# A recommendation model's pair products: eight bursts of 32 small matmuls a part become four of 64

## The reference

```python
fm = emb_table[jnp.arange(N_CAT)[None, :], cat_idx]
h = jax.nn.relu(dense_x @ Wd1 + bd1)
h = jax.nn.relu(h @ Wd2 + bd2)
dense = jax.nn.relu(h @ Wdf + bdf)
Z = jnp.concatenate([fm, dense[:, None, :]], axis=1)
S = jnp.einsum('bie,bje->bij', Z, Z)
iu, ju = np.triu_indices(N_CAT + 1, k=1)
x = jnp.concatenate([S[:, iu, ju], dense], axis=-1)
x = jax.nn.relu(x @ Wt1 + bt1)
x = jax.nn.relu(x @ Wt2 + bt2)
x = jax.nn.relu(x @ Wt3 + bt3)
x = jax.nn.relu(x @ Wt4 + bt4)
return jax.nn.sigmoid(x @ Wo + bo)
```

## Time and profile before

| | us |
|---|---|
| median of 3 runs (635.88 to 641.29) | 639.12 |
| the profiled execution | 634.22 |
| its span, first to last instruction | 632.2 |
| PE busy, share of the span | 569.1, 90% |
| POOL busy, share of the span | 402.9, 64% |

### The profile page before, as it was taken

The page is one execution under the profiler, slowest core; times in us unless marked ns, Lnnn a source line. Parts: engine busy times, 40 slices in busy tenths (PEclk is TensorE's granted clock), DMA queues, the critical chain, the costliest instruction groups (busy, mean ns, idle before and its releaser), DMA issues.

```text
span 632.2 us, 17990 instructions
## 1 busy us (share of the span) xinstructions
PE 569.1 (90%) x8112; PEld 537.1 (85%) x8112; DVE 211.9 (34%) x438; ACT 241.3 (38%) x506; POOL 402.9 (64%) x421
## 2 busy tenths in 40 slices
PE   0995078989899999999999999999999999999988
PEld 0774068989799999989998999999999999999987
DVE  6754235532342224322331334132423143214111
ACT  1864134434342334333432444243424243424222
POOL 5877777777777777777777777777777776000000
PEclk9999578989899999999999999999999999999999
DMA  6644736995338643683359434863376346500430
GB/s 122 174 118 88 182 52 151 315 338 133 55 54 239 203 57 54 165 276 54 54 76 320 98 55 54 272 170 54 54 237 204 55 55 179 205 2 3 185 148 1
DMA packets 36309, 83.93 MB, mean 133 GB/s; under 512 B 8086, under 2 KB 23966, under 8 KB 30678
## 3 DMA queue, kind: packets, MB, share of 16 engines
q0 software_dynamic: 13312, 27.29, 26.3%
q1 hardware_dynamic: 22360, 55.30, 25.3%
q10 hardware_dynamic: 562, 0.20, 0.2%
HBM read 74.37 MB, written 8.40 MB: 131 GB/s over the span
## 4 chain that ended last, share of the span: by engine, by line
PE 51%; POOL 32%; issue 10%; DMA 5%; DVE 1%; ACT 1%; DVEq 0%
PE acc L714 40%; POOL gathered L491 32%; PE bank L745 5%; DMA wt<-split_t 3%; PE unit L762 3%; DMA gathered<-table,row_of 1%; PE acc L724 1%; PE unit L776 1%; ACT h L625 0%; DVE feats L499 0%; DVE h L553 0%; ACT acc L626 0%; DVE unit L500 0%; DVE feats L498 0%; ACT h L622 0%
## 5 line engine op out<-in xcount | busy, mean ns | idle before, releaser
L491 POOL DMA_INDIRECT gathered<-table,row_of x416 | 402.2, 967 | 130.8 <-issue 126.4
L714 PE MATMUL acc<-h,wt 128*128 128x256 f32 (+1 forms) x2568 | 342.6, 290 | 10.0 <-DVE h L553 5.1
L714 PEld LDWEIGHTS acc<-h,wt 128*128 128x128 f32 x2568 | 319.7, 192 | 17.9 <-DVE h L553 6.4
L625 ACT ACTIVATE h<-acc,bias 128x256 fp32r<-128x256 f32 (+1 forms) x104 | 51.1, 491 | 239.0 <-PE acc L714 239.0
L553 DVE TENSOR_TENSOR h<-acc,h 128x256 fp32r<-128x256 f32 (+1 forms) x104 | 46.3, 445 | 277.3 <-ACT acc L626 262.7
L714 PE MATMUL acc<-x,wt 126*128 126x256 f32 (+2 forms) x768 | 97.1, 286 | 1.6 <-DVE h L550 1.5
L714 PEld LDWEIGHTS acc<-x,wt 126*128 126x128 f32 (+2 forms) x768 | 94.0, 193 | 5.3 <-issue 3.1
L745 PE MATMUL bank<-eye,gathered 128*128 128x128 f32 x416 | 52.5, 279 | 20.0 <-DMA gathered<-table,row_of 20.0
L745 PEld LDWEIGHTS bank<-eye,gathered 128*128 128x128 f32 x416 | 47.9, 144 | 21.0 <-DMA gathered<-table,row_of 20.5
L658 ACT ACTIVATE feats<-bank 128x512 f32<-128x512 f32 (+1 forms) x56 | 56.0, 1095 | 16.3 <-PE bank L745 16.2
L571 DVE COPY feats<-bank 128x512 f32<-128x512 f32 (+1 forms) x56 | 55.2, 1057 | 9.6 <-PE bank L745 9.6
(11 more groups left out here) (44 smaller groups left out, 171.8 us busy)
## 6 DMA issues: line engine op xcount, KB each, us to landing
wt<-split_t SPq DMA_DIRECT2D x35, 1024.0 KB
raw<-w_t SPq DMA_DIRECT2D x17, 512.0 KB, 4.7
split_t<-wt SPq DMA_DIRECT2D x8, 1024.0 KB, 9.4
gathered<-table,row_of POOLq DMA_INDIRECT x416
raw<-w_d SPq DMA_DIRECT2D x1, 512.0 KB, 4.3
feats<-xT SPq DMA_DIRECT2D x4, 104.0 KB
rows<-idx SPq DMA_DIRECT2D x1, 208.0 KB, 2.6
raw<-w_df SPq DMA_DIRECT2D x1, 128.0 KB, 5.0
```

The costliest lines, as they stand in the source:

```text
L491: nc.gpsimd.indirect_dma_start(gathered[:, t % SLOTS, c, :], None, table, bass.IndirectOffsetOnAxis(row_of[:, t, c:c + 1], 0)).then_inc(ga ...
L625: nc.scalar.activation(parts[0], source, ACT.Relu, bias=b)
L714: mm = nc.tensor.matmul(result, strip[0:height, a, k, :], given[0:height, b, k, :], start=(n == 0 and (a, b) == (0, 0)), stop=(n == len(bl ...
```

## The change

Only the table `NEXT_AT` changes. In each list the four half units of a tile take two places instead of four: both halves of a unit stand before the same strip. In the general list (stretches 2 to 6) the first tile's half units stood before strips 9, 10, 11 and 12 and now stand before 9, 9, 12 and 12; the second tile's stood before 16, 17, 18 and 19 and now before 15, 15, 18 and 18, and the second tile's flips move from 14 and 15 to 13 and 14. In stretches 0 and 1 the flips keep their places. The number of instructions with work in them stays the same on every engine.

```diff
-NEXT_AT = [(6, 8, 9, 10, 11, 12, 14, 15, 16, 17, 18, 19, 20, 21, 22, 22) for _ in PARTS]
-
-NEXT_AT[0] = (9, 10, 12, 13, 14, 15, 19, 20, 21, 22, 22, 22, 22, 22, 22, 22)
-NEXT_AT[1] = (8, 9, 10, 11, 12, 13, 15, 16, 17, 18, 19, 20, 21, 21, 22, 22)
+NEXT_AT = [(6, 8, 9, 9, 12, 12, 13, 14, 15, 15, 18, 18, 20, 21, 22, 22) for _ in PARTS]
+
+NEXT_AT[0] = (9, 10, 12, 12, 15, 15, 19, 20, 21, 21, 22, 22, 22, 22, 22, 22)
+NEXT_AT[1] = (8, 9, 10, 10, 13, 13, 15, 16, 17, 17, 20, 20, 21, 21, 22, 22)
```

## The result

The changed kernel is slower: 645.76 us (median of 4 runs) against 638.13 us (4 runs), 7.6 us or 1.2% apart; the ratio on record, an estimate of its own, is 1.0175 with a 95% interval of 1.0128 to 1.0222. The slowest of the four runs before took 641.29 us, the quickest of the four after 645.00. The forecast was no change, 642.0 us. Runs marked slow on record (two of e9's, 798.23 and 2964.64 us, and one of e10's, 650.82 us, among them) are left out of every ratio and of the medians of e9 and e10.

The account below looks back on a forecast made before the run. PE's list of matmuls was taken to bound the kernel, behind a wait for tile 7's gather until 280.30 us. The terms summed to +3.2 us; with the median before taken as 639.1, the forecast was 642 us, range 634 to 649.

Parts of the forecast that it names:

- tile 7's flip starts at 280.30: In stretch 2, PE waits for tile 7's last gather; the start was to stay at 280 ± 1 us.
- 1. strip 13 behind the gate: At tile 7 PE reaches the flip a strip earlier, waits longer and still has strip 13 to do: +2.9 us.
- the gate: PE's wait for tile 7's last gather, to 280.30 us; savings ahead of it were to be lost in waiting.
- 2. switches: Going from strips to pairs and back, saved for 18 bursts behind tile 7's flip at 0.26 us each: −4.7 us.
- 3. waits for strip 15's result: In stretches 3 and 5 strip 16 waits in full, no longer covered by a burst: +1.6 us.
- 4. waits for t2's weights: PE's waits for these loads behind tile 7's flip change by −0.4 us; bounds −1.4 and +1.4.
- 5a: PE's instruction packets run out in long bursts: two or three waits of 0.8 us, +2.0 us.
- 5b: Slower pace inside bursts of 128 records: 0.1 us each over 18, +1.8 us; bounds 0 and 0.7 us each.
- The condition given: For a wait, an instruction packet must begin within some 12 records of a burst's start: about one burst in five.
- the instruction supply: Rival: every second of the 18 merged bursts on PE runs dry for 1.2 us; about 649 us, chance 0.22.
- The case against it: Against the supply rival: 24 to 72 strips, 3 to 9 us, stand between bursts, time in which packets come.
- the gate's rival: Tile 7's gather lands up to some 4 us earlier and all 26 merges count: about 634 us, chance 0.10.

Follow-up runs that it names:

- e9: Kernel before, with half units standing in pairs in stretch 6 alone: 639.51 us against 635.61, ratio 1.0064.
- e10: The changed kernel run once more for a second profile: 642.88 us against 635.61 for the kernel before, ratio 1.0159.
- e4: Changed kernel without the loads of t2's weights from stretch 3 on: 636.33 us, executed once.
- e2: Kernel before, with only the second tile's flips and half units moved earlier in the general list, nothing merged: 638.41 us, ratio 1.0037.
- e12: e9 without five 1 MB loads of t2's weights, meant for stretch 6 but in fact those of stretch 7: 639.46 us.
- e6: Changed kernel with gathers from tile 10 on bringing 32 numbers a row instead of 128, as many transfers: 644.07 us, executed once.
- e5: Changed kernel with POOL running an iota into an idle buffer in place of each gather from tile 10 on: 631.39 us, executed once.
- e13: e9 without the ten 1 MB loads of t2's weights in stretches 6 and 7: 637.19 us.

## Why the prediction was wrong

Its six terms, against the two profiled executions of the changed kernel, each less the one of before. Terms 1 and 2 stand at their forecast size; each was checked at single places only:

| term | forecast | after | e10 |
|---|---|---|---|
| tile 7's flip starts at 280.30 | 0 | +0.7 | −1.1 |
| slow transposes and strip at the flip | – | +1.6 | +0.1 |
| 1. strip 13 behind the gate | +2.9 | +2.9 | +2.9 |
| 2. switches, 18 × 0.26 | −4.7 | −4.7 | −4.7 |
| 3. waits for strip 15's result | +1.6 | +1.3 | +1.3 |
| 4. waits for t2's weights | −0.4 | −1.2 | −0.6 |
| 5a. instruction blocks | +2.0 | +5.8 | +2.5 |
| 5b. pace inside bursts | +1.8 | +6.2 | +5.5 |
| sum | +3.2 | +12.6 | +5.9 |
| the spans differ by | | 13.0 | 5.9 |

**The step that failed is 5b, "I take 0.1 us each".** It is the term of the sum that was mis-sized: the bounds were 0 and 0.7; it is (27.5 − 21.3) / 18 = 0.34 in the mean and (1.62 − 1.10) = 0.5 for most of the 14 beside gathers. The row was in the profile: at 1.62 / 127 = 12.8 ns a record the bursts of 128 are like those of 98, 148 and 176 in the earlier trace rows, at 11 to 14 ns, and not like those of 64. I set them aside because they stood amid loads and, two of them, in slices with a lowered clock. The trace of before says otherwise of the three bursts themselves (start and end, us, PE busy and its records, granted clock, DMA share, GB/s):

```profile
55.60:58.12 2.52, 2.42 (x176) 1.00 0.45 68
85.23:87.50 2.27, 2.14 (x148) 1.00 0.39 52
164.38:165.68 1.30, 1.30 (x99) 1.00 0.29 47
```

The granted clock was full, 1.00, in all three, the lowered stretches of those slices lay elsewhere, and the queue of the weights moved nothing in any of them. Nor do the loads slow a burst (e4). But all three stood beside POOL's gathers, which go on to about 535 us. What I took for a mark of the first parts was a mark of the length, beside gathers.

With 5b at its 6.2 us and the other terms as forecast, the sum would be 3.2 + 4.4 = 7.6 us, just what the medians differ by. That it fits so closely is luck, as terms 3, 4 and 5a came out otherwise too.

**Term 5a varies too much to be judged from two profiles.** In after there was one wait of 3.6 and one of 0.5 us, where before had 0.4 in all, and the strip behind the long one took 5.03 us instead of 2.97:

```profile
479.01 1.50 PE L762 MATMUL unit<-feats 128*27 128x26 f32 x91
484.12 0.67 PE L762 MATMUL unit<-feats 128*27 128x26 f32 x37 [3.61 <-issue]
484.72 5.19 PE L714 MATMUL acc<-h,wt 128*128 128x256 f32 x24
```

In e10 there were 2.9 us of waits in four places. But e2, which merges nothing, had 3.8 us of them from 285 us on, so how much of this the change adds isn't shown. What the runs do show is the size of one wait: up to 3.6 us, not 0.8, and the lowered clock behind it added 2.1 us (after) and 2.4 us (e9). The condition given, a block that begins within some 12 records of a burst's start, fits e9, where it would have begun a few records ahead of the burst; but the wait in after's burst at 479 came behind its 91st record, with more than 30 records of strips in the same block.

**The other terms held.** A clean cycle took 10.03 us (term 2). Strip 16 waited 1.45 us at 364.23 us in stretch 3 instead of 0.79:

```profile
364.23 5.98 PE L714 MATMUL acc<-h,wt 128*128 128x256 f32 x48 [1.45 <-DVE h L553]
```

The weights came no later (term 4). Term 1's price fits what e2 measured (+2.4 us, 0.2 to 4.5), and the flip started at 280 ± 1 us, as forecast; the longer wait at the gate did not come, because PE came to it late.

**Of the rivals** the instruction supply decided, with 649 us for 645.76 measured. Its sum was near, but its mechanism only in part: it priced the bursts running dry every second time for 1.2 us, while 14 of 18 were interrupted one to three times for mostly 0.2 to 0.28 us by a cause, the issue of gathers, that neither the forecast nor the rival named. The case against it, that strips between the bursts give packets time to come, does not hold for these pauses, and not always for the blocks: after's 3.6 us stood behind three strips. Of the gate's rival the premise came true in one execution, e10's, where the gate did not hold PE; its time did not, 640.1 us being still above before's.

**Still open:** why issuing an indirect transfer stops PE's supply at two places of each; what is shared was not tried. Nor was it tried what lowers the clock behind a long wait: e9 and after had it, e2 after 1.82 us too, e12 with 2.43 us did not. And single executions vary by some 8 us (640.08 to 648.62 for the change in e10's runs); late blocks are one cause that is seen, whether the only one is not known.

## What to carry to other kernels

Before small matmuls are put side by side to save switches, read the pace of the longest bursts that the profile already has, and ask what else runs at that time: if there is a slower pace from some length on, that length is the price. While GpSimd issues indirect transfers, keep runs of tiny matmuls short enough to end before the first pauses (here 64 records mostly did) and put long-running ones between them. A whole instruction block in one run beside large loads can cost several us once, so a merged place is to be timed where its block falls, not by its switch.

## What the runs showed of the hardware

- While POOL issued an indirect transfer every 1.25 us, long bursts of small matmuls stood still at two places of each 1.25 us, for 0.2 to 0.28 us; a quarter of the bytes (e6: 27.4 against 27.5 us for 18 bursts) and POOL busy with other work (e5: 21.5 us) showed that neither bytes nor a busy POOL matter. A burst's first 32 records went at 7 ns, later ones at 8.4, and no pause stood before about the 45th.
- At the same record of the same burst PE stood still for 3.63 and 2.43 us beside loads of 1 MB (e9, e12) and not at all without them (e13). In bursts of 64 such waits were 1.82 and 2.27 us (e2, e13).
- Switching from strips to pair products and back costs about the same for long bursts as for short ones: a cycle of a burst of 128 behind the gathers has 10.03 − 3 × 2.91 − 127 × 8.7 ns = 0.2 us of it, one of 64 had 0.26.
